# Four PSUM banks instead of two for the last 48 half-steps of an attention, with its weighted sums issued two half-steps later

## The reference

```
q = (src @ Wq + bq).reshape(B, T, N_HEAD, HEAD_DIM)      # B=4, T=512, 16 heads of 16
k = (src @ Wk + bk).reshape(B, T, N_HEAD, HEAD_DIM)
v = (src @ Wv + bv).reshape(B, T, N_HEAD, HEAD_DIM)
scores = jnp.einsum('bqhd,bkhd->bhqk', q, k) * scale
probs = jax.nn.softmax(scores, axis=-1)
attn = jnp.einsum('bhqk,bkhd->bqhd', probs, v).reshape(B, T, D_MODEL)
attn = attn @ Wo + bo
x = _layer_norm(src + attn, ln1_g, ln1_b)
keys = (x @ router_w + router_b)[..., 0]
expert_idx = jnp.remainder(jnp.floor(keys).astype(jnp.int32), N_EXPERTS)
# each token then passes through its expert (256 -> 1024 -> 256), a second layer norm and a gated residual
```

## Time and profile before

| | us |
|---|---|
| median of 3 runs | 580.56 (577.52 to 580.72) |
| the profiled execution's own time | 580.17 |
| its span, first to last instruction | 578.1 |
| last residual addition of batch 2 on VectorE (L693) ends at | 331.3 |
| score 208, the first of the last 48 half-steps, starts at | 332.45 |
| the last weighted sum starts at | 384.80 |
| last output projection, TensorE | 389.40 to 395.09, at 1.2 GHz until 393.4 |
| routing and gather | to 421 |
| expert loop, 11 slots | 421 to 578 |

### The profile page before, as it was taken

The page is one execution under the profiler, slowest core; times in us unless marked ns, Lnnn a source line. Parts: engine busy times, 40 slices in busy tenths (PEclk is TensorE's granted clock), DMA queues, the critical chain, the costliest instruction groups (busy, mean ns, idle before and its releaser), DMA issues. The chain is left out here.

```text
span 578.1 us, 8313 instructions
## 1 busy us (share of the span) xinstructions
PE 482.5 (83%) x2535; PEld 278.8 (48%) x2535; DVE 390.9 (68%) x871; ACT 244.9 (42%) x483; POOL 207.4 (36%) x273
## 2 busy tenths in 40 slices
PE   3985999989999999999987789864289998988960
PEld 2542443343334444433422332213289888988960
DVE  4655579796789895789798698017966555555651
ACT  1021016563445462446566254453055444544530
POOL 3153005030025124034033375412345555555651
PEclk9996779998989986989999795557579999998995
DMA  7637521643474523437647800200111211111220
GB/s 222 141 94 254 132 33 43 244 139 94 78 109 169 195 85 103 108 44 182 190 110 189 159 21 1 76 0 1 54 37 36 64 56 54 55 40 53 64 54 19
DMA packets 40127, 54.99 MB, mean 95 GB/s; under 512 B 12686, under 2 KB 24476, under 8 KB 40093
## 3 DMA queue, kind: packets, MB, share of 16 engines
q1 hardware_dynamic: 34272, 38.37, 26.7%
q0 software_dynamic: 5328, 15.74, 8.5%
q10 hardware_dynamic: 492, 0.47, 0.3%
HBM read 36.73 MB, written 17.83 MB: 94 GB/s over the span
## 5 line engine op out<-in xcount | busy, mean ns | idle before, releaser
L588 ACT ACTIVATE probs<-sc 128x512 f32<-128x512 f32 x256 | 141.4, 595 | 173.1 <-PE sc L892 170.1
L736 DVE TENSOR_REDUCE mx<-amax 128x1 f32<-128x512 f32 x256 | 166.6, 678 | 47.2 <-PE amax L883 47.1
L892 PE MATMUL sc<-QS,KS 50*128 50x512 f32 x256 | 108.1, 502 | 14.9 <-ACT probs L588 12.5
L883 PE MATMUL amax<-KS,QS 48*128 48x512 f32 x256 | 106.9, 500 | 11.0 <-DMA KS<-qk_dram 6.2
L892 PEld LDWEIGHTS sc<-QS,KS 50*128 50x128 f32 x256 | 43.7, 202 | 115.9 <-ACT probs L588 56.1
L883 PEld LDWEIGHTS amax<-KS,QS 48*128 48x128 f32 x256 | 42.0, 197 | 28.0 <-DVE mx L736 13.8
L1247 PE MATMUL amax<-W_hi,hid_hi 128*128 128x256 f32 x160 | 48.2, 301 | 4.2 <-DVE hid_lo L1147 3.8
L526 POOL TENSOR_TENSOR an<-av,rec 128x256 f32<-128x256 f32 x16 | 10.2, 637 | 102.8 <-DVE rec L725 102.7
L1247 PE MATMUL amax<-W_hi,hid_lo 128*128 128x256 f32 x160 | 46.7, 292 | 0.0
L1247 PE MATMUL amax<-W_lo,hid_hi 128*128 128x256 f32 x160 | 46.5, 291 | 0.0
L904 PE MATMUL pv<-probs,V1b 128*32 128x512 f32 x256 | 44.8, 780 | 1.4 <-ACT probs L588 1.2
(11 more groups left out here) (220 smaller groups left out, 897.0 us busy)
## 6 DMA issues: line engine op xcount, KB each, us to landing
qk_dram<-HL SPq DMA_DIRECT2D x16, 512.0 KB, 3.9
QS<-qk_dram SPq DMA_DIRECT2D x90, 64.0 KB, 3.2
KS<-qk_dram SPq DMA_DIRECT2D x90, 64.0 KB, 3.1
W_sb<-in_L_ffn_W SPq DMA_DIRECT2D x8, 512.0 KB, 4.3
xc<-in_x SPq DMA_DIRECT2D x4, 512.0 KB, 3.6
xc<-in_ctx SPq DMA_DIRECT2D x4, 512.0 KB, 4.6
x_dram<-xc POOLq DMA_DIRECT2D x4, 512.0 KB, 3.5
res_dram<-t_a POOLq DMA_DIRECT2D x4, 512.0 KB, 3.9
```

The costliest lines, as they stand in the source:

```text
L588: nc.scalar.activation(probs[:, n % 8, c * 512:(c + 1) * 512], sc[c][:, :], ACT.Exp, scale=SCALE).then_inc(exp_done, 1)
L736: nc.vector.reduce_max(mx[:, to:to + 1], amax[m % 3][:, :], AX.X).then_inc(max_done, 1)
L883: nc.tensor.matmul(amax[m % 3][:, :], QS[rows, pair, chunk * P:(chunk + 1) * P], KS[rows, pair, :], start=True, stop=True).then_inc(A_full, 1)
L892: nc.tensor.matmul(sc[c][:, :], KS[rows, pair, kc * P:(kc + 1) * P], QS[rows, pair, :], start=True, stop=True).then_inc(sc_full, 1)
```

## The change

From half-step 208 on the scores turn over four banks, `sc[0], sc[1], side[0], side[1]`, in place of two. `score(u)` then waits for the exponentials of `u - 4` in place of `u - 2`; 208 and 209 keep the old wait, and 210 and 211, which write the side banks for the first time, wait for `r_done` = 6 (both residual additions of batch 2) in place of `exp_done`. The weighted sums of four half-steps are issued 7 behind in place of 5, so the ones that stood at `u` = 209, 213, ... 257 stand at 211, 215, ... 259. Before the last output projection TensorE waits for all 256 exponentials, since the side banks held scores.

```diff
+        def score_bank(u):
+
+            return (sc + side)[u % 4] if u >= WIDE else sc[u % 2]
...
+        WIDE, PV_AFTER_WIDE = 208, 7
...
-                nc.scalar.activation(probs[:, n % 8, c * 512:(c + 1) * 512], sc[c][:, :], ACT.Exp, scale=SCALE).then_inc(exp_done, 1)
+                nc.scalar.activation(probs[:, n % 8, c * 512:(c + 1) * 512], score_bank(u)[:, :], ACT.Exp, scale=SCALE).then_inc(exp_done, 1)
...
-                wait(pe, exp_done, u - 1)
+                if WIDE + 2 <= u < WIDE + 4:
+                    pe.wait_ge(r_done, B * 2 - 2)
+                else:
+                    wait(pe, exp_done, u - 1 - 2 * (u >= WIDE + 4))
                 rows, pair = rows_of(c, 50), 2 * (g % G) + u // 2 % 2
-                nc.tensor.matmul(sc[c][:, :], KS[rows, pair, kc * P:(kc + 1) * P], QS[rows, pair, :], start=True, stop=True).then_inc(sc_full, 1)
+                nc.tensor.matmul(score_bank(u)[:, :], KS[rows, pair, kc * P:(kc + 1) * P], QS[rows, pair, :], start=True, stop=True).then_inc(sc_full, 1)
...
-                r = u - PV_AFTER
+                r = u - (PV_AFTER_WIDE if u >= WIDE else PV_AFTER)
                 if r % 4 == 0 and 0 <= r < END:
                     weighted_values(r // 4)
...
+            pe.wait_ge(exp_done, END)
             for i in range(2):
                 for half in range(2):
                     side_work("O", i, half, B - 1)
```

## The result

The changed kernel takes 564.38 us, median of 4 runs (560.46 to 573.12), against 579.04 for the kernel before in the same comparison (4 runs, 576.44 to 580.72). The ratio is 0.9718, 95% interval 0.967 to 0.9766: faster, by 16.3 us of 579 (13.5 to 19.1); the two medians lie 14.7 us apart. The ratios here leave out every execution that took over 1.5% longer than the fastest of its kernel, of these four the one of 573.12. The forecast was 572, the range began at 564.5, and the rival in which the clock comes back had been priced at 566 to 568, or 565 where it never falls.

What follows compares the result with a forecast made beforehand. The two-bank ring was taken to bound half-steps 232 to 255, VectorE those before. From 360.6, five rounds of 3.19 us put the last sums at 376.5 instead of 384.80: 8.3 us less, 572 us; range 564.5 to 577.

Steps and rivals of the forecast that it cites:

- the rival in which the clock comes back: Half-steps 232 to 255: denser TensorE work restores 2.4 GHz, ScalarE becomes the bound; 566 to 568 us, chance 0.38.
- where it never falls: Last 48 half-steps: clock stays full throughout, the load holds half-step 240 at 362.9; 565 us, range's low end 564.5.
- The forecast holds 1.2 GHz to the end, as before: Half-steps 232 to 255: TensorE's clock assumed to stay at 0.50 as in the earlier profile; chance of the forecast 0.48.
- three signs of being wrong: Clock 1.00 after 363, `av` showing a wait before 357, or half-step 240 waiting for `QS`.
- The ring of two banks: Half-steps 232 to 255: scores wait for their bank's exponentials, so four half-steps take 4.56 us.
- The round of four at the low clock: Half-steps 232 to 255 with four banks: 0.60 + 0.72 + 1.87 = 3.19 us in place of 4.56.
- The first two parts: Half-steps 208 to 221 and 222 to 231: VectorE stays the limit; gives two half-steps and costs 0.5 us.
- The place where I had TensorE past half-step 235: TensorE and its sums there at 360.6, where before it was past 233 at 360.06.
- The load for group 15: Half-step 240: load ready at 362.9, needed at 363.8; free at this pace, the next limit at a faster one.
- `r_done`: Wait at half-step 210 for batch 2's additions, ended at 331.3: free; 0.7 us once if late by one VectorE operation.
- the rival of the low clock in it: Expert loop: low clock reaches in, a slot's 11.3 us would double; slot and a half makes 589 us, chance 0.05.
- four exponentials at 2.26 us: Half-steps 240 to 255 at full clock: ScalarE as bound, 16 x 0.565 = 9.0 us, last sums ending at 374.7.

Runs made afterwards that it cites:

- second profile of the change: The changed kernel, unaltered, run and profiled again: 565.97 us (6 runs) against 580.92 for the kernel before, ratio 0.9744.
- the two from 232 on: The changed kernel with both edits from half-step 232 on instead of 208, run on two chips: 562.56 us, ratio 0.9698, and 568.1, ratio 0.9748.
- Keeping the clock up: Against the kernel with both edits from half-step 232 on (568.1): two unread matmuls added after each pair, half-steps 212 to 230; 573.04 us, ratio 0.984.

## Why the prediction was wrong

**The step that failed.** "The forecast holds 1.2 GHz to the end, as before." It wasn't so: in both profiles of the changed kernel the clock was at 2.4 GHz for most of the last 24 half-steps (0.80 and 0.86). I had that as a rival with 0.38 against 0.48, and weighed against it that 10.21 us in flight of 11.09 had not brought the clock back. That was the wrong row to weigh: in that stretch TensorE still stood between its rounds, and the weight loads that I took to stay uncovered left no gap here. With both edits, low stretches from score 232 on hold TensorE in flight 3.90 of 3.90 us (second profile of the change), 6.51 of 6.51 and 10.67 of 10.90 (the two from 232 on), and each ends at 2.4 GHz. The two-bank kernel with added matmuls shows that the full clock is worth 6.6 us there. The banks alone, whose rounds still hold 0.75 us of waiting, show that the direction of an edit is not enough: at 3.83 us a round the clock stayed down; with rounds of 3.0 to 3.5 it came back in every profile. Of the three signs of being wrong, the clock came true in both profiles, and half-step 240 waited for `QS` in both (2.21 us, and 0.85 for the weight load); `av` waited once, 0.98 us at 358.44 in the second.

**What held.** The ring of two banks is what bounded the last 24 half-steps, and both edits are needed to lift it. The round of four at the low clock was put at 3.19 us and measured 3.00 where it was steady, since the sums followed the second pair by 0.56 (374.42 to 374.98) and not by 0.72; with the banks alone 3.83 was worked out and 3.84 and 3.83 measured. The first two parts gave nothing: 24.05 and 26.45 us with the change, 24.5 and 24.4 without. That VectorE's reductions hold them fits the first profile (21.91 of 24.05); in the second TensorE was in flight 25.37 of 26.45 at the low clock and was the limit itself. The place where I had TensorE past half-step 235, 28.15 us behind score 208, came 25.71 and 29.46 us behind it; from there to the last sums I had 15.9, and it took 15.57 and 11.11. So the first profile gained its extra microseconds ahead of that place and lost some at half-step 240, the second gained them behind it. The later sums alone are worth nothing. The load for group 15 is the next limit at the fast pace: the wait at 240 is there, 2.21 us in the first profile. `r_done` cost nothing. The expert loop is unchanged, 150.0 against 150.5, and the rival of the low clock in it is refuted.

**What was mis-sized beside it.** With the clock back I priced four exponentials at 2.26 us from the row at 338.88, in which ScalarE was fed by two banks: its first pair starts at 338.88, its second not before 340.06. Fed by four it does four in 1.93 to 2.15. Over 16 half-steps that is 8.16 us (366.91 to 375.07) in place of 9.0, 0.9 us that the rival's price lacked. The other part is behind the start of the last sums: they take 1.07 us in place of 1.94, and the output projection 5.38 and 5.25 in place of 5.69 and 5.93; the rest up to the end came out 1.7 to 3.0 us shorter in all. Forecast 8.3; with the clock and these, 12.7 to 14.5 by the profiles and 13.5 to 19.1 by the times. Whether the last 1 to 2 us are more than the spread of the executions stays open: score 208 alone started anywhere from 329.0 to 345.2 in the profiles of this study, with nothing changed ahead of it.

The median of 564.38 lies 0.12 us under the range, which ended at the case that the clock never falls. It fell in both profiles, so the time came there by another road than the one priced. Part of it is not the change at all: the range stands on 580.56 for the kernel before, whose median in the comparison was 579.04, 1.5 us lower. Set against the profiled 580.17, the 12.7 to 14.5 us of the profiles give 565.7 to 567.5, about the 566 to 568 of the rival. That the median fell just outside and not just inside the range is chance; that the forecast of 572 was too slow is not, and its cause is the clock.

## What to carry to other kernels

Where an engine's clock follows its load, price a wait that is taken away twice: once at the clock of the profile before, and once at the clock that the denser work may bring back. If the first price holds the old clock, say what row makes it stay. A ring of buffers and the distance at which its reader is issued are one edit: here four banks gave half, the distance nothing, both 2.8%. And take an engine's price per operation from start to start in a run that is never held up, not from the length of a merged row, which can hide waits. An experiment that is to lift a clock needs a ground in which the clock is low.

## What the runs showed of the hardware

Adding matmuls that nobody reads made the two-bank kernel 1% faster (0.9863 to 0.9937), with TensorE at a mean clock of 0.87 where it was 0.50. Beside it stands that the banks alone, 23.93 us for 24 half-steps with TensorE in flight 18.73 of them, stayed at 1.2 GHz throughout, and that the whole change did not. Falls came behind short stalls: in the first profile of the changed kernel TensorE's matmuls stood 2.21 us at half-step 240, and the clock was at 0.50 within 1.3 us of going on; in the kernel of "Keeping the clock up" they stood 2.36 us there, and the clock fell in that wait. In the five other profiles with both edits that wait was 0.53 us at most, and a clock once back stayed up to the last sums. That the stall is what lets it fall was not tried by itself. The Trainium skill (TensorE: Matmul & The Clock Gate, "What's actually happening") says that activity lifts a clock that rests at the lower level; the runs agree, with 21.2 us in place of 27.8 for the same 24 half-steps where matmuls were added. The report of the Trainium skill (same page, "HAM oscillation") that double-buffering PSUM brought nothing further does not carry over: here going from two banks to four gave half of the gain by itself.
